# Broadcasts, Gram sums and the first chunk's spread on TensorE in a selective-scan block

## The chip, the cores and the metric

The kernel runs on one core of a Trainium2 chip. The metric is the device time of one execution in microseconds (us), the median of several runs.

## The reference

The input x is 8 batches of 96 channels by 64 x 64 positions (4096 tokens a batch). Two layers are computed:

```
u = group_norm(x, 32 groups)
xm, z = u @ in_proj.T                              # 192 channels each
xm = silu(causal depthwise conv of 4 taps (xm) + conv_b)
dt, Bm, Cm = xm @ x_proj.T                         # 6, 16 and 16 columns
delta = softplus(dt @ dt_proj_w.T + dt_proj_b)
h_t = exp(delta*A) * h_(t-1) + delta*u*Bm_t        # 192 channels x 16 states, over 4096 tokens
y_t = sum over states (h_t * Cm_t) + xm*D ;  x = x + layer_norm((y*silu(z)) @ out_proj.T)
t = x + attention(layer_norm(x))                   # without softmax, so through a Gram matrix
out = t + ffn(layer_norm(t))                       # hidden 384, operands in fp8, sums in f16
```

## The kernel before

**Tiling.** The 4096 tokens of each batch are 8 chunks of T = 512 tokens, so there are 64 chunks, numbered g = 0 to 63. The place of a chunk is g mod 8. The recurrence runs with 128 partitions = 32 channel groups x 4 states: the 192 x 16 pairs are 24 scans of 128 x 512 a chunk (L1277), in 6 quads s = 0 to 5 of 4 scans each. Quads 0 to 3 hold the "low" 128 channels, quads 4 and 5 the "high" 64.

**The work of one chunk.** ScalarE (ACT) computes a decay DA = exp(ds*A) for each scan (`decay`, L840) into one of two PSUM banks, so decay j can start only when scan j-2 is done. The scan's input D = us * B comes from `inputs`: VectorE (DVE) makes it for quads 0, 1 and part of 3 (L1261), GpSimd (POOL) for quads 2, 4, 5 (L649) and for the rest of quad 3 (`rest`, L658). SPLIT = 232 is the column at which quad 3 is divided. D has three buffers. Where DVE makes it, B stands in the PSUM bank PB, to which ACT copies it (`put_b`, L826, three copies a chunk). POOL then multiplies the scanned rows R with C (`product`, L676 and L672) and makes du = delta*u (L642). TensorE (PE) sums over the states into bank Y (`sum_states`, L1645 and L1649) and adds the skip (`add_skip`, L1656 and L1659); DVE gates (`gate`, L1298, in two halves).

**Through memory.** delta and du (tiles dl, du) and B, C (tile st) are produced on channel or state partitions, but the scans need them repeated over partitions. The DMA queue of SyncE (SP) writes them to scratch arrays in memory (lo_d, hi_d, bc_d) and reads them back repeated, into ds, us, Bs and Cs.

**Stages overlap.** An iteration g of every engine's program holds the scans of chunk g, the front of chunks g+1 and g+2 (norm, conv, `silu`, `x_proj`, `state_rows` L802 that copies x_proj's result from PSUM to st with a bias, `dt_proj`, `parts` L811, `softplus` L815, `delta` L1287), the layer norms of g-1 and g-2 (L851, L855, `scale_out` L1302, `token_norm` L1310), the Gram matrix of chunk g-2 (`gram`: PE multiplies the tokens tT with themselves, L1715, and DVE adds the result in bank G2 to tile G, L1336), and from g = 10 on the feed-forward of chunk g-10. One batch behind, `fold` turns the Gram sum into the attention's matrix. Each engine's order is written out by hand in `iteration`; semaphores tie them.

**The order that the change touches.** In iteration g, ACT goes: ... `decay(g,1,1)` (quad 1, scan 1), `decay(g,1,2)`, `state_rows(g+1)`, `decay(g,1,3)`, `output` (L929), `decay(g,2,0)`, two `parts`, `decay(g,2,1)`, `put_b(g,3)`, `softplus(g+1)`. DVE goes: `scan(g,0,0)`, `gate(g-1,0)`, `token_norm`, `scan(g,0,1)`, `inputs(g,1)`, `scan(g,0,2)`, `gate(g-1,1)`, `scan(g,0,3)`, `scan(g,1,0..2)`, `gram(g-2)`, `scan(g,1,3)`, `scan(g,2,0..1)`, `delta(g+1)`. PE goes: `add_skip(g-1,1)` (which waits for the first gate, L1659), `x2_tokens`, `sum_states(g-1,4)`, `sum_states(g-1,5)`, `to_tokens`, `x_proj(g+1)`, `down`, `gram(g-2)`, `dt_proj(g+1)`, `out_proj(g-1)`.

**The first chunk.** Nothing hides its front. ACT makes the low delta at 25 us, DVE clamps it (`delta`), SP writes it to lo_d as soon as it is there (L472, with semaphores low_out), POOL makes du, SP writes it too and reads both back spread (L488).

Of the kernel before, what the change touches and what calls it, by code (L numbers as in the profile page):

```python
# [9 lines left out]
T = 512  # L10
# [37 lines left out]
SPLIT = {3: 232}  # L48
# [8 lines left out]
def build(nc, I, cols, out):  # L57
# [7 lines left out]
    with ctx:  # L65
# [95 lines left out]

        once = pieces(stage[:, 1024:1024 + I["once"].shape[1]], cols["once"])
# [9 lines left out]
        wz, cb, dsk, wx, one_row, dtw = (W[n] for n in ("wz_in", "conv_b", "D", "wx", "one_row", "dtw"))  # L172
# [4 lines left out]
        off_group, of_group = W["off_group"], W["of_group"]  # L177
        wqT, wkv, wfT, b1f, b2f = (W[n] for n in ("wqT", "wkv", "wffT", "b1", "b2"))
        wcv = sb("wcv", [C, TAPS, 2 * LOW])
# [20 lines left out]
        un = sb("un", [C, HALO + T])  # L200
# [4 lines left out]
        st = sb("st", [128, T])  # L205
# [13 lines left out]
        sq = sb("sq", [C, T])  # L219
# [14 lines left out]
        fsq = sb("fsq", [C, T])  # L234
# [11 lines left out]
        w_in, w_rest, once_in, cwb_in = sem("w_in"), sem("w_rest"), sem("once_in"), sem("cwb_in")  # L246
# [5 lines left out]
        passed = sem("passed")  # L252
        x_in, xq_in = sem("x_in"), sem("xq_in")
# [4 lines left out]
        u_in = [sem("u_in0"), sem("u_in1")]  # L258
        first_quad = sem("first_quad")
# [4 lines left out]
        low_out = [sem("dl_low_out"), sem("du_low_out")]  # L264
# [9 lines left out]
        z_kept = sem("z_kept")  # L274
# [16 lines left out]
        post_dve = Progress("post_dve", 3)  # L291
# [104 lines left out]
        def _(sp_eng):  # L396
# [7 lines left out]
            sp_eng.dma_start(kept_w[:, 0:soon], I["kept"][:, 0:soon]).then_inc(w_in, 16)  # L404
            sp_eng.dma_start(stage[:, 1024:1024 + I["once"].shape[1]], I["once"]).then_inc(once_in, 16)
            sp_eng.dma_start(cwb, I["conv_w"].partition_broadcast(C)).then_inc(cwb_in, 16)

            def load_front(k):
                if there(k - 1):
                    sp_eng.wait_ge(front_mm.sem, front_mm.at(k - 1))  # L410
                    own_wait(sp_eng)
                t, lo = place(k) * T, 0 if place(k) == 0 else HALO
                sp_eng.dma_start(un[:, HALO - lo:HALO + T], I["x"][batch(k), :, t - lo:t + T]).then_inc(x_in, 16)
# [29 lines left out]
            def spill_bc(k):  # L443
                sp_eng.wait_ge(st_done.sem, st_done.at(k))
                if there(k - 2):
                    for n in range(2):
# [3 lines left out]
                                 st[32:32 + 2 * STATE, :]).then_inc(bc_out, 16)  # L450
# [30 lines left out]
            def spread(k, w, n, dst, landed):  # L481
                p = place(k) % 2
                if k == 0 and n == 0:
                    sp_eng.wait_ge(low_out[w], 16)
                else:
                    sp_eng.wait_ge(sp_out[w], count(k, 48, 48))
# [64 lines left out]
            def iteration(g):  # L551
# [5 lines left out]
                if there(g + 2):  # L557
                    load_front(g + 2)
# [11 lines left out]
                if there(g):  # L570
                    load_c(g, 1)
                if there(g + 1):
                    spill_bc(g + 1)
                    if g == -1:
                        load_b(0, 0)
                if ahead(g + 11):
                    load_stats(g + 11)
                if there(g + 1):
                    if g == -1:
                        first_spills()  # L580
                    else:
                        spill(g + 1, 0)
                        spill(g + 1, 1)
                    if g >= 0:
# [4 lines left out]
                    if g >= 0:  # L589
                        spread_delta(g + 1, 0)  # L590
                    load_b(g + 1, 1)
                    if g == -1:
                        load_c(0, 0)
# [28 lines left out]
        def _(pool):  # L622
            credit(nc.gpsimd, by_pool)

# [8 lines left out]
            def delta_u(k):  # L633
                if k == 0:
                    return first_delta_u()
                if k == 1:
                    pool.wait_ge(low_out[1], 16)
# [41 lines left out]
            def iteration(g):  # L679
                if there(g - 1):  # L680
                    product(g - 1, 5)
                if there(g):
                    if g == 0:
                        inputs(0, 1, first_quad)
# [26 lines left out]
        def _(act):  # L711
# [59 lines left out]
            def norm(k):  # L771
# [4 lines left out]
                if lo:  # L776
                    act.wait_ge(front_mm.sem, front_mm.at(k - 1))
                    nc.scalar.copy(un[:, 0:HALO], zero[0:C, 0:HALO])
                nc.scalar.activation(un[:, lo:], un[:, lo:], ACT.Identity, bias=cgs[:, 1:2],
                                     scale=cgs[:, 0:1]).then_inc(normed.sem, 1)  # L780

            def silu(k, *src):
# [14 lines left out]
            def state_rows(k, src):  # L797
                act.wait_ge(back_mm.sem, back_mm.at(k, 1))
                act.wait_ge(back_mm.sem, back_mm.at(k - 1))
                if there(k - 1):  # L800
                    act.wait_ge(bc_out, count(k - 1, 16, 16))
                nc.scalar.activation(st[:, :], src[:, :], ACT.Identity, bias=one_row).then_inc(st_done.sem, 1)  # L802

            def parts(k, v, src):
# [4 lines left out]
                if k == 1:  # L809
                    act.wait_ge(low_out[0], 16)  # L810
# [5 lines left out]

            def put_b(k, s):
                if k == 0 and s == 1:
                    return
                h, w = LOWS[s]  # L820
                if s == 3 and place(k + 3) == 0 and later(k + 3):
                    act.wait_ge(gn_act.sem, gn_act.at(k + 3, 4))
# [1398 lines left out]
```

## Time and profile before

| | |
|---|---|
| runs | 2509.95, 2510.44, 2512.78 us; median 2510.44 us |
| profiled execution, span from first to last instruction | 2508.8 us (its own device time is not listed; span and median lie 1.6 us apart) |
| granted TensorE clock, mean | 0.987 |
| busy PE, DVE, ACT, POOL | 2142.1, 2454.5, 2314.7, 2414.8 us |
| idle POOL before its first large operation | to 27.07 us |
| DMA | 494.54 MB, 197 GB/s |

A row of the timeline gives start, length, engine, line, operation, written tile <- read tiles, shapes and count; the bracket is the idle time of the engine before it and what ended it. The records of consecutive instructions on DVE, ACT and POOL overlap, so what one costs its engine is the distance from its start to the next start, somewhat less than its length.

### The profile page before, as it was taken

To read this page: it belongs to the slowest core of one execution; us is meant where nothing else is said; L and a number is where in the kernel's file an instruction comes from. 1 tells how busy PE (TensorE), PEld (TensorE's weight loads), DVE (VectorE), ACT (ScalarE), POOL (GpSimd) and SP (SyncE) were. 2 spreads that over 40 slices of the span, in tenths; PEclk is the share of its full clock that TensorE was granted. 3 is DMA by queue.
4 is the path that set the end of the run, shared out by engine and by line. 5 is a ranking of instruction groups with operands and counts; after the bars stand their busy time and mean duration, and the time that the engine had idled before them with its cause. 6 is when DMAs were issued, how large, how long until landed. Compare 5 with 4: busy or idle time off the path is not lost.

```text
span 2508.8 us, 35019 instructions
## 1 busy us (share of the span) xinstructions
PE 2142.1 (85%) x10314; PEld 826.0 (33%) x10314; DVE 2454.5 (98%) x2391; ACT 2314.7 (92%) x3960; POOL 2414.8 (96%) x655
## 2 busy tenths in 40 slices
PE   6788888888888888888888888888888888888878
PEld 3334434323323323323333323323323333333323
DVE  7999999999999999999999999999999999999986
ACT  5777777999999999999999999999999999999977
POOL 4999999999999999999999999999999999999991
PEclk8999999999999999999999999999999999999979
DMA  6555555556656656566566566566566565566542
GB/s 243 189 185 172 195 185 184 202 198 207 209 202 205 207 201 212 201 205 206 204 206 214 194 208 212 195 210 208 198 210 211 197 207 201 192 206 203 186 142 75
DMA packets 171388, 494.54 MB, mean 197 GB/s; under 512 B 23072, under 2 KB 44704, under 8 KB 154240
## 3 DMA queue, kind: packets, MB, share of 16 engines
q1 hardware_dynamic: 171200, 492.30, 57.9%
q8 instruction: 85, 1.39, 0.2%
q14 instruction: 103, 0.84, 0.1%
HBM read 400.33 MB, written 91.88 MB: 196 GB/s over the span
## 4 chain that ended last, share of the span: by engine, by line
POOL 40%; issue 40%; DVE 15%; PE 3%; ACT 1%; DMA 0%; POOLq 0%; DVEq 0%; SPq 0%; ACTq 0%
POOL R L676 20%; DVE R L1277 11%; POOL D L649 9%; POOL R L672 7%; POOL du L642 3%; DVE D L1261 2%; POOL D L658 2%; PE G L1568 1%; PE Y L1568 0%; DVE q L1357 0%; DVE dl L1287 0%; DVE G L1302 0%; DVE h L1471 0%; DVE h L1478 0%; PE Y L1645 0%
## 5 line engine op out<-in xcount | busy, mean ns | idle before, releaser
L1277 DVE TENSOR_TENSOR_SCAN R<-DA,R,D 128x512 f32<-128x512 f32 x1344 | 1630.2, 1263 | 1.0 <-ACT DA L840 1.0
L840 ACT ACTIVATE DA<-ds,kept_w 128x512 f32<-128x512 f32 x1536 | 1054.8, 688 | 139.9 <-DVE R L1277 127.1
L676 POOL TENSOR_TENSOR R<-R,Cs 128x2048 f32<-128x2048 f32 x255 | 970.9, 3819 | 4.0 <-DVE R L1277 2.6
L649 POOL TENSOR_TENSOR D<-us,Bs 128x2048 f32<-128x2048 f32 x193 | 736.9, 3818 | 8.8 <-DMA us<-lo_d 8.8
L672 POOL TENSOR_TENSOR R<-R,Cs 128x4096 f32<-128x4096 f32 x64 | 476.5, 7446 | 0.1
L1261 DVE TENSOR_TENSOR D<-us,PB 128x2048 f32<-128x2048 f32 x191 | 356.8, 1868 | 6.3 <-DMA us<-lo_d 6.3
L1645 PE MATMUL Y<-R,kept_w 128*32 128x512 f32 x2048 | 266.1, 615 | 13.9 <-POOL R L672 12.8
L1602 PE MATMUL G<-un,wcv 96*128 96x512 f32 x512 | 251.6, 614 | 29.5 <-ACT h L907 29.5
L1277 DVE TENSOR_TENSOR_SCAN R<-DA,D 128x512 f32<-128x512 f32 x192 | 221.7, 1204 | 2.1 <-ACT DA L840 2.1
L1605 PE MATMUL G<-un,wcv 96*64 96x256 f32 x1024 | 138.5, 392 | 60.1 <-ACT xq L888 58.9
L1568 PE MATMUL G<-st,kept_w 128*64 128x256 f32 (+1 forms) x384 | 108.9, 485 | 53.5 <-ACT st L802 53.5
L1602 PEld LDWEIGHTS G<-un,wcv 96*128 96x128 f32 x512 | 87.9, 189 | 187.8 <-issue 113.8
L1568 PE MATMUL G<-sq,kept_w 96*96 96x512 f32 (+1 forms) x256 | 136.7, 616 | 13.5 <-DVE dl L1287 12.6
L1649 PE MATMUL Y<-R,kept_w 128*32 128x256 f32 x2048 | 136.9, 385 | 5.9 <-POOL R L676 5.9
L658 POOL TENSOR_TENSOR D<-us,Bs 128x1120 f32<-128x1120 f32 x64 | 139.2, 2174 | 0.0
L1568 PE MATMUL G<-q,w1q 96*128 96x512 fp8e5 x164 | 62.7, 386 | 77.1 <-DVE q L1357 44.7
L911 ACT ACTIVATE h<-h,b1q 128x512 f16<-128x512 f16 x165 | 117.1, 711 | 0.0
L1605 PEld LDWEIGHTS G<-un,wcv 96*64 96x64 f32 x1024 | 62.3, 135 | 147.6 <-ACT xq L888 111.1
L1568 PE MATMUL G<-un,kept_w 96*64 96x256 f32 x372 | 107.9, 470 | 0.0
L1645 PEld LDWEIGHTS Y<-R,kept_w 128*32 128x32 f32 x2048 | 47.8, 110 | 168.3 <-issue 107.3
L642 POOL TENSOR_TENSOR du<-dl,u 128x768 f32<-128x768 f32 x63 | 97.6, 1549 | 0.0
L826 ACT COPY PB<-Bs 128x512 f32<-128x512 f32 x191 | 95.2, 498 | 0.0
(240 smaller groups left out, 3437.5 us busy)
## 6 DMA issues: line engine op xcount, KB each, us to landing
Bs<-bc_d SPq DMA_DIRECT2D x128, 512.0 KB, 5.6
us<-lo_d SPq DMA_DIRECT2D x64, 1024.0 KB, 6.3
ds<-lo_d SPq DMA_DIRECT2D x64, 1024.0 KB, 8.4
Cs<-bc_d SPq DMA_DIRECT2D x128, 512.0 KB, 4.7
us<-hi_d SPq DMA_DIRECT2D x64, 512.0 KB, 6.8
ds<-hi_d SPq DMA_DIRECT2D x64, 512.0 KB, 5.5
lo_d<-dl SPq DMA_DIRECT2D x64, 256.0 KB, 2.0
lo_d<-du SPq DMA_DIRECT2D x64, 256.0 KB, 2.0
```

Of the source, the lines that this page charges most:

```text
L642: nc.gpsimd.tensor_tensor(du[:, :], dl[:, :], u[:, place(k) % 2, :], ALU.mult)\
L649: nc.gpsimd.tensor_tensor(shaped(D[:, s % NDBU, :, :], s), low(us, s) if s in LOWS else high(us), of_states(Bs, s), ALU.mult).then_inc(don ...
L658: nc.gpsimd.tensor_tensor(D[:, s % NDBU, :, cs], us[:, 0:QUAD, cs], Bs[:, h, w, cs].unsqueeze(1).to_broadcast([128, QUAD, T - SPLIT[s]]), ...
L672: nc.gpsimd.tensor_tensor(R[:, s:s + 2, :, 0:T], R[:, s:s + 2, :, 1:S], Cs[:, 1, :, :].unsqueeze(2).to_broadcast([128, 2, QUAD, T]), ALU.m ...
L676: nc.gpsimd.tensor_tensor(shaped(R[:, s, :, 0:T], s), shaped(R[:, s, :, 1:S], s), of_states(Cs, s), ALU.mult).then_inc(hc_done.sem, 1)
L840: nc.scalar.activation(DA[j % NDA][:, :], ds[:, i, :], ACT.Exp, scale=A[:, j:j + 1]).then_inc(exp_done.sem, 1)
L1261: nc.vector.tensor_tensor(D[:, s % NDBU, :, 0:n], us[:, 0:QUAD, 0:n], PB[:, 0:n].unsqueeze(1).to_broadcast([128, QUAD, n]), ALU.mult)\
L1277: nc.vector.tensor_tensor_scan(R[:, s, q, 1:S], DA[j % NDA][:, :], D[:, s % NDBU, q, :], before, ALU.mult, ALU.add).then_inc(scanned.sem, 1)
L1568: return mm(o, left, right, start=True, stop=True)
L1602: last = mm(o[:, :], wcv[:, t, 0:LOW], un[:, t:t + T], start=(t == 0), stop=(t == TAPS - 1))
L1605: last = mm(o[rows, 0:H], wcv[:, t, LOW:LOW + HIGH], un[:, t + cs.start:t + cs.stop], start=(t == 0), stop=(t == TAPS - 1))
L1645: last = mm(Y[32 * q:32 * q + 32, :], sumsel, R[:, s, q, 0:T], start=s == 0, stop=s == 3)
```

## The change

1. `put_b` moves from ACT to PE: instead of copying the spread B from Bs, PE multiplies a selection matrix `bsel` (32 x 128) with the 32 state rows of st into PB. st gets two buffers, and its rows are laid out anew (B and C in rows 0 to 31, dt in rows 32 to 63, ones in row 64).
2. Four biases leave ACT: conv_b becomes a 97th row of the conv's first tap, the epsilon of the layer norms a 97th row of avg, and dt_proj's row of ones is set once, so `silu`, the Ln of L851 and L898, and `state_rows` run without a bias tile.
3. `gram`: PE first adds the old sum (identity `id97` times G) in PSUM, and ACT copies the result to G, behind `decay(g,1,2)`; DVE's addition goes (it stays for the last two chunks).
4. SPLIT: 232 becomes 248.
5. Chunk 0: low delta and du are spread by PE with 8 matmuls against four blocks of a selection matrix (`spread_first`), and ACT copies each result to ds or us; the two early spills and the two spreads through memory go. DVE makes D of quad 0 scan by scan. Quad 1's D is POOL's, as before. z of chunk 0 gets its Silu early, `silu(1)` moves behind `decay(0,1,1)`, `z_proj(1,0)` into iteration 0, and two of the six statistics of batch 2 behind `scan(0,2,1)`. SP's order at the start follows.

```diff
-SPLIT = {3: 232}
+SPLIT = {3: 248}
...
 # SyncE
+            sp_eng.dma_start(wcv[C:C + 1, 0, :], I["conv_b"]).then_inc(cb_in, 16)
...
-                for w, low_done, src in ((0, dl_low, dl), (1, du_low, du)):
-                    sp_eng.wait_ge(low_done, 1)
-                    sp_eng.dma_start(lo_d[0, w].rearrange("e i t -> (e i) t"), src[:, part(0)]).then_inc(low_out[w], 16)
...
                     if g == -1:
                         load_b(0, 0)
+                        load_b(0, 1)
...
-                    spread_du(g + 1, 0)
-                    if g == -1:
-                        spread_delta(0, 0)
...
 # ScalarE
-                nc.scalar.activation(st[:, :], src[:, :], ACT.Identity, bias=one_row).then_inc(st_done.sem, 1)
+                nc.scalar.copy(st[0:64, k % 2, :], src[0:64, :]).then_inc(st_done.sem, 1)
...
-            def put_b(k, s):
...
-                nc.scalar.copy(PB[:, 0:n], Bs[:, h, w, 0:n]).then_inc(b_put.sem, steps_to(k, s))
...
+            def gram(k, src):
+                act.wait_ge(post_mm.sem, post_mm.at(k, 6))
+                if place(k) == 0 and there(k - CH):
+                    act.wait_ge(fold_mm.sem, fold_mm.at(k - CH, 1))
+                nc.scalar.copy(G[:, :], src[0:C + 1, 0:C + 1]).then_inc(gram_kept.sem, 1)
...
                 if there(g):
                     decay(g, 1, 2)
+                if there(g - 2) and g - 2 < LAST - 1:
+                    gram(g - 2, G2)
                 if there(g + 1):
                     state_rows(g + 1, G3)
...
+                keep_ds(0, 1, Y)
                 decay(0, 0, 0)
+                keep_us(0, 2, G2)
+                keep_ds(1, 3, G3)
+                decay(0, 0, 1)
+                keep_us(1, 4, G0)
+                keep_us(2, 5, Y)
+                keep_us(3, 6, G2)
+                keep_ds(2, 7, G3)
+                decay(0, 0, 2)
+                keep_ds(3, 8, G0)
...
 # VectorE
+            def first_inputs(q):
...
+                nc.vector.tensor_tensor(D[:, 0, q, :], us[:, q, :], PB[:, :], ALU.mult)\
+                    .then_inc(first_d if q + 1 < QUAD else dbu_d.sem, 1)
...
-                if there(g - 2):
-                    gram(g - 2, G2)
...
+                if g == 0:
+                    stats(2, gx_in[3:4], range(4, 6))
...
 # TensorE
             def gram(k, o):
+                more = place(k) > 0 and k < LAST - 1
+                if more:
+                    pe.wait_ge(gram_kept.sem, gram_kept.at(k - 1))
+                    mm(o[0:C + 1, 0:C + 1], id97, G[:, :], start=True, stop=False)
...
+            def put_b(k, s):
...
+                pe.wait_ge(st_done.sem, st_done.at(k))
+                pe.wait_ge(dbu_d.sem, dbu_d.at(k, BY_DVE[s] - 1))
+                n = SPLIT.get(s, T)
+                one(PB[:, 0:n], bsel[:, BY_DVE[s] - 1, :], st[0:2 * STATE, k % 2, 0:n]).then_inc(b_put.sem, 1)
...
+                if there(g):
+                    put_b(g, 1)
                 if there(g - 1):
                     add_skip(g - 1, 1)
...
                     out_proj(g - 1, G1)
+                if there(g):
+                    put_b(g, 3)
...
                     variance(g - 1, 1, G2)
+                if there(g + 1):
+                    put_b(g + 1, 0)
...
+                put_b(0, 0)
...
+                pe.wait_ge(dl_low, 1)
+                spread_first(dl, 0, Y)
+                pe.wait_ge(du_low, 1)
+                pe.wait_ge(w_ready, 1)
+                spread_first(du, 0, G2)
+                spread_first(dl, 1, G3)
...
+            def spread_first(src, q, o):
+                one(o[:, :], of_block[:, q, :], src[:, part(0)]).then_inc(picked, 1)
```

## Rows read from the trace of the kernel before

**Rows 1.** Busy time by engine, chunks 11 to 60 (columns: stretch, length, engines, clock, DMA)

```profile
core 0: us, PE busy (x) PEld busy (x) DVE busy (x) ACT busy (x) POOL busy (x), PEclk, DMA share, GB/s
380.00:2390.00 2010.00, 1732.14 (x8393) 646.71 (x8381) 2007.10 (x1908) 1952.32 (x3354) 2006.90 (x537) 1.00 0.60 203
```

**Rows 2.** DVE's waits: from 120 to 430 us, and from 430 to 1500 us

```profile
DVE yv L1298 <- PE Y L1649: 3.3, 7, 0.8
...
DVE G L1302 <- ACT rs L855: 1.0, 4, 0.2
```

**Rows 3.** POOL's timeline: the same operation of chunks 40 and 48, a batch apart

```profile
1518.95 1.54 POOL L642 TENSOR_TENSOR du<-dl,u 128x768 f32<-128x768 f32 x1
...
1819.38 1.55 POOL L642 TENSOR_TENSOR du<-dl,u 128x768 f32<-128x768 f32 x1
```

**Rows 4.** Groups by shape from 500 to 2000 us (busy us, mean ns of one)

```profile
L1261 DVE TENSOR_TENSOR D<-us,PB 128x2048 f32<-128x2048 f32 x80 | 180.6, 2258 | 0.0
...
L649 POOL TENSOR_TENSOR D<-us,Bs 128x2048 f32<-128x2048 f32 x120 | 458.5, 3821 | 0.0
```

**Rows 5.** DVE's timeline in iteration 43, a common one

```profile
1662.61 0.23 DVE L1336 TENSOR_TENSOR G<-G 97x97 f32<-97x97 f32 x1
1662.76 3.62 DVE L1277 TENSOR_TENSOR_SCAN R<-DA,R,D 128x512 f32<-128x512 f32 x3
```

**Rows 6.** ACT's timeline in the same iteration

```profile
1660.37 0.69 ACT L840 ACTIVATE DA<-ds,kept_w 128x512 f32<-128x512 f32 x1 [0.46 <-DVE R L1277]
1661.00 0.67 ACT L802 ACTIVATE st<-G,kept_w 128x512 f32<-128x512 f32 x1
1661.57 0.68 ACT L840 ACTIVATE DA<-ds,kept_w 128x512 f32<-128x512 f32 x1
...
1664.15 0.69 ACT L840 ACTIVATE DA<-ds,kept_w 128x512 f32<-128x512 f32 x1
1664.76 0.36 ACT L826 COPY PB<-Bs 128x232 f32<-128x232 f32 x1
1665.04 0.85 ACT L815 ACTIVATE dl<-dl 128x768 f32<-128x768 f32 x1
```

**Rows 7.** PE's timeline in the same iteration

```profile
1650.40 1.13 PE L1568 MATMUL G<-un,kept_w 96*128 96x512 f32 x2
1652.55 0.65 PE L1659 MATMUL Y<-u,kept_w 64*64 64x256 f32 x4 [1.02 <-DVE yv L1298]
...
1660.19 0.85 PE L1715 MATMUL G<-tT 128*97 128x97 f32 x8
```

**Rows 8.** Groups of ACT by shape from 500 to 2000 us: copies and small operations from PSUM

```profile
L888 ACT COPY xq<-G 96x512 f32<-96x512 f32 x40 | 23.8, 594 | 0.0
...
L744 ACT ACTIVATE gt<-PB 96x1 f32<-96x1 f32 x5 | 0.8, 159 | 0.0
```

**Rows 9.** Timelines of PE and of DVE in iteration 40, place 0

```profile
1547.67 0.85 PE L1715 MATMUL G<-tT 128*97 128x97 f32 x8
...
1549.80 0.23 DVE L1336 TENSOR_TENSOR G<-G 97x97 f32<-97x97 f32 x1
```

**Rows 10.** Timelines of PE and of DVE in iteration 45, place 5

```profile
1735.71 0.91 PE L1715 MATMUL G<-tT 128*97 128x97 f32 x8
...
1737.73 0.23 DVE L1336 TENSOR_TENSOR G<-G 97x97 f32<-97x97 f32 x1
```

**Rows 11.** PE's timeline at the start

```profile
24.91 0.57 PE L1568 MATMUL PB<-kept_w 96*97 96x192 f32 x2
```

**Rows 12.** DVE's timeline at the start

```profile
26.30 1.02 DVE L1287 SCALAR_TENSOR_TENSOR dl<-dl,G 128x512 f32<-128x512 f32 x2
...
37.55 2.29 DVE L1261 TENSOR_TENSOR D<-us,PB 128x2048 f32<-128x2048 f32 x1 [6.31 <-DMA us<-lo_d]
40.72 10.14 DVE L1277 TENSOR_TENSOR_SCAN R<-DA,D 128x512 f32<-128x512 f32 x9 [0.89 <-ACT DA L840]
```

**Rows 13.** POOL's timeline at the start

```profile
37.59 7.59 POOL L649 TENSOR_TENSOR D<-us,Bs 128x2048 f32<-128x2048 f32 x2 [8.84 <-DMA us<-lo_d]
...
55.05 1.55 POOL L642 TENSOR_TENSOR du<-dl,u 128x768 f32<-128x768 f32 x1
```

More of the change, by code:

```diff
@@ L482, in spread @@
                 p = place(k) % 2
[L483 to L486, printed above, removed]
+                sp_eng.wait_ge(sp_out[w], count(k, 48, 48))
                 if n == 0:
@@ L556, in iteration @@
                     load_c(g, 0)
-                if there(g + 2):
+                if there(g + 2) and g != 0:
                     load_front(g + 2)
@@ L787, in silu @@
                     act.wait_ge(front_mm.sem, front_mm.at(k, FRONT[v]))
-                    nc.scalar.activation(u[:, place(k) % 2, part(v)], src[v], ACT.Silu, bias=cb[:, v:v + 1])\
+                    nc.scalar.activation(u[:, place(k) % 2, part(v)], src[v], ACT.Silu)\
                         .then_inc(silued.sem, 1)
@@ L935, in iteration @@
             def iteration(g):
-                if there(g):
-                    put_b(g, 1)
+                if there(g) and g > 0:
                     decay(g, 0, 1)
@@ L940, in iteration @@
                     inv_std(g - 2, 1)
-                if there(g):
+                if there(g) and g > 0:
                     decay(g, 0, 2)
@@ L1031, in iteration @@
                     decay(g, 5, 0)
-                if there(g + 1):
-                    put_b(g + 1, 0)
                 if g == LAST:
@@ L1096, in beginning @@
                     act.wait_ge(front_mm.sem, front_mm.at(0, 1 + v))
-                    last = nc.scalar.activation(u[:, 0, part(v)], src[:, 0:T - H * v], ACT.Silu, bias=cb[:, v:v + 1])
-                    last.then_inc(silued.sem, 1)
+                    nc.scalar.activation(u[:, 0, part(v)], src[:, 0:T - H * v], ACT.Silu).then_inc(silued.sem, 1)
+                for v in range(2):
+                    act.wait_ge(front_mm.sem, front_mm.at(0, 3 + v))
+                    nc.scalar.activation(z[:, 0, part(v)], DA[v][:, 0:T - H * v], ACT.Silu).then_inc(silued.sem, 1)
                 nc.scalar.preload_act_table_set(EXP_LN)
@@ L1101, in beginning @@
                 state_rows(0, G0)
-                for v in range(2):
-                    act.wait_ge(front_mm.sem, front_mm.at(0, 3 + v))
-                    nc.scalar.copy(z[:, 0, part(v)], DA[v][:, 0:T - H * v]).then_inc(z_kept, 1)
                 norm(1)
@@ L1202, in stats @@
                     dve.wait_ge(gn_aggr.sem, gn_aggr.at(CH * n - CH))
-                for c in range(ROW // T):
+                for c in blocks:
                     if c % per == 0:
@@ L1374, in iteration @@
                     scan(g, 0, 1)
+                if there(g) and g > 0:
                     inputs(g, 1)
+                if there(g):
                     scan(g, 0, 2)
@@ L1419, in iteration @@
                     scan(g, 5, 1)
-                if there(g + 1):
+                if there(g + 1) and g >= 0:
                     inputs(g + 1, 0)
```

243 lines of the change are left out of this document (138 added, 105 removed).

## The prediction

> **What bounds the kernel now.** First the busy time by engine of the long middle: POOL and DVE are both busy 2007 of 2010 us, ACT 1952, PE 1732, at full clock [rows 1]. Neither of the two waits for memory, so the question is which sets the pace. The waits answer it by stretch: up to chunk 10 DVE stalls at its gate L1298, seven times and 3.3 us in all, for sums that wait for POOL's products; from there on its only waits are 1.0 us in 29 chunks, for ACT's rs [rows 2]. So POOL sets the pace of some 11 chunks and DVE that of the 53 behind them. The distance of one POOL operation over a batch says how close it is: 1819.38 - 1518.95 = 300.4 us [rows 3], where eight chunks in which POOL never waits would take about 299.5 (its seven of 3.8, the pair and the two small ones, 37.44 each).
>
> At the start nothing of this holds: DVE waits 6.31 us and POOL 8.84 us for us from memory, and POOL's unbroken work begins at 37.59 [rows 12, 13].
>
> **The third engine** matters because DVE waits for its decays. In a common iteration ACT idles 0.46 us before the decay at 1660.37, since there are two banks [rows 6]; from that point its order is tied to DVE's scans. Its next decay starts at 1661.57 and ends at 1662.25, and the scan that reads it starts at 1662.76, behind the Gram addition [rows 5, 6]. The slack is 0.5 us. The change takes 0.15 of it from DVE's side and puts a wait for PE into ACT's.
>
> **The change, part by part.** I sum against the profiled execution's span, 2508.8 us; the same difference is then laid on the median, 2510.4.
>
> *Split at 248.* 16 columns of 4 rows, 64 elements, go from POOL to DVE. By [rows 4] an element costs POOL 3821/2048 = 1.87 ns and DVE 2258/2048 = 1.10 ns: -0.12 us for POOL, +0.07 for DVE, each chunk.
>
> *Gram addition off DVE.* From its start to the next start it costs 0.15 us [rows 5]. With the split: -0.08 us a chunk for DVE.
>
> *Gram sum on PE and ACT.* PE adds two passes of 97 columns; eight take 0.85 us, the record of one alone being about 0.25, so 0.086 each, +0.17 [rows 7]. PE's Gram product ends at 1661.04 and would end at 1661.21; ACT, free at 1661.00, would begin to copy at 1661.25 (about 0.04 between the engines, estimated from the gaps of such rows). The copy of 97 columns appears nowhere: it is above one of 1 column (record 0.16) and below one of 512 (0.59) [rows 8]; consecutive records overlap by 0.1, and on the line between both it takes 0.24 - 0.1 = 0.14, ends 0.06 and 0.49. I take 0.13. `state_rows` follows at 1661.38. It costs 0.57 now (1661.00 to 1661.57); without a bias tile it is a copy like L888, whose record is 0.59 against 0.67, so 0.48. Then the decay starts at 1661.86, ends at 1662.55, and the scan could start at 1662.58; DVE without its addition gets there at 1662.61. No stall. Two decays on, ACT has no pause any more: in the present row it takes 2.58 us from decay to decay (1661.57 to 1664.15), of which about 0.1 is a wait that goes, so the decay at 1664.15 would start at 1664.32, and its scan at 1665.05. DVE gets there at 1664.97 (two scans of 1.18 behind 1662.61): a stall of **0.07 us** in a common chunk, which eats nearly all of the 0.08.
>
> That ACT is quicker without the bias is also what the Trainium skill says (ScalarE: Activation LUTs, What ACT_TABLE_LOAD costs): a [128,1] pointer operand adds some 93 ns. The rows agree (0.67 against 0.59). By the page's slope of 0.833 ns a column and the 51 ns it gives for PSUM (Perfetto Trace Analysis, Optimizing Scalar/DVE Operations) the copy of G would be an estimated 0.13 us; the sum above does not need it.
>
> *The same reading elsewhere in a batch.* Place 0: scans without a carried start are 0.05 shorter, the product ends at 1548.52, the addition stood at 1549.80 [rows 9]: 1548.52+0.17+0.04+0.13+0.48+0.73 = 1550.07, a stall of 0.27, and 0.21 more two decays on; 0.48. Place 5: group-norm matmuls for the next batch stand ahead of the product, which ends at 1736.62; 1738.17 against 1737.73 is 0.44 [rows 10], and with the small Ln behind it and the second stall 0.67. For places 1 and 2, whose product is late by less, I put 0.3 and 0.2. With four common chunks at 0.07 that is **1.9 us a batch** (ends: 0 if ACT copies while PE is early, and 3 if the copy takes 0.25).
>
> *B on PE.* The three copies leave ACT; one stands between decay and softplus, 0.28 us from start to start [rows 6]. DVE's waits for rs, 1.0 us in 29 chunks [rows 2], should vanish with it and the cheaper Ln: -0.3 us a batch. PE gains two pairs of 512 columns and one of 248, and its queue is the question. The nearest row is a pair that starts at 1650.40; PE stands idle 1.02 us up to 1652.55, waiting for DVE's gate [rows 7]. A pair of 1.0 us ahead of `add_skip` fills that idle time to within 0.1. `put_b(g,3)` (0.45) delays a variance that waits for DVE anyhow, `put_b(g+1,0)` stands before two waits of PE for ACT of 0.5 us each. I take 0 for all, ends 0 and +0.25 a chunk.
>
> *The first chunk.* Now: `put_b(0,0)` goes ahead of the fold's matmul at 24.91 [rows 11], for which DVE waits before its clamp, so delta moves from 26.30 to about 27.3 [rows 12]. Then come eight pairs on PE at 1.0 us from about 28.2, each followed by an ACT copy of about 0.55, with three decays of 0.7 between. The last piece of us is the seventh thing ACT does, after PE's sixth pair (34.3): us is whole at about 35.0. POOL begins there and not at 37.59: -2.6. DVE begins its scans at about 32 instead of 40.72 but then loses 3.6 us, since `silu(1)` and its two table loads (1.28 us each) now stand between two decays; this lies beside POOL's two large operations (7.6 us [rows 13]). `delta(1)` moves behind two statistics and is late by some 0.6 for POOL's L642 at 55.05. Left: **-2.2 us** (ends: -0.5, if us waits on B's load or PE is slower; -3.5). The spills and spreads saved were 2.5 MB that nobody else waited for.
>
> *Sum.* Start -2.2. 11 chunks at POOL's pace, -0.12 each: -1.3. 53 chunks, 6.6 batches, at DVE's: -0.08 x 53 = -4.2; waits for rs -2.0; stalls for ACT +1.9 x 6.6 = +12.5. Together +2.8 us. The end of the kernel is as before: its last two Gram additions stay on DVE. 2510.4 + 2.8 = 2513.2, **2513 us**.
>
> **Rivals.** *(A) No new stall worth naming.* If ACT's copy slips in while PE's product is early, or the decay chain has more play than I read, the 12.5 us fall to 0 to 5: 2510.4 - 2.2 - 1.3 - 4.2 - 2.0 = 2500.7, up to 2505. For it: the common chunk misses by only 0.07; ACT loses 1.3 us of copies and 0.5 us of biases a chunk. Against it: places 0 and 5 miss by 0.3 and more. *(B) PE's queue, slower.* `put_b(g,1)` stands ahead of `add_skip(g-1,1)`, and from there to the Gram product PE has no pause. Should the pair cost over 1.1 us (weights not loaded in time, for instance), every tenth beyond delays both the second gate and ACT's copy. At +0.25 us a chunk over 53 chunks: +13, 2525; it decides from 1.1 us on, and +0.1 gives 2518. For it: the idle time is 1.02 us, no more. Against it: pairs in this stretch follow each other at 1.0. *(C) The start brings nothing*, since POOL's early work is tied to scans behind `silu(1)`: 2514.5; inside the forecast.
>
> **How the numbers follow.** A measurement of this kernel tells 0.2%, 5 us, from no change. The forecast and C, 2505.5 to 2515.5: 0.45 (C 0.07 of it). Rival A, below: 0.33. B, or stalls near 3 us a batch (2520), above: 0.22. Neither side alone can be left out; the range reaches to A's time and to B's lower half: 2500 to 2519.
>
> **What would show it.** In the changed profile: ACT's L802 (now a copy) 0.09 shorter, and about 0.4 us later behind its decay; DVE's waits with "R <- ACT DA" of about 0.07 in common chunks, 0.3 or more at places 0 and 5, some 12 us in all; POOL waiting for DVE's scans 2 to 3 us a batch; a batch 0.9 us longer than 300.4 (-0.66 - 0.3 + 1.9); us whole at 35 and POOL's first L642 near 52.8. No such DVE waits, and batches near 299.5, would be A. PE without its idle time before L1659, and DVE waiting for L1649, would be B.

## The result, and the profile after

| | before | after |
|---|---|---|
| median of 4 runs each (us) | 2510.39 (2509.95 to 2512.78) | 2529.90 (2527.32 to 2534.85) |
| ratio | | 1.0077, interval 1.0062 to 1.0091 |
| profiled execution: span | 2508.8 | 2526.5 (its device time 2528.29) |
| a batch in the steady part (defined below) | 300.43 | 302.77 |

The change makes the kernel slower by 0.8%, and the time lies above the predicted range. (Before now has a fourth run, 2510.34 us, beside the three listed above.) Below, a batch is always the distance between the starts of DVE's `token_norm` of chunks 24 and 56, divided by four. Lines have moved: the decay is L825, the scan L1290, `scale_out` L1315, the Ln and Exp of rs L836 and L840, the selection products of `put_b` L1582 with PB.

The busy time of the long middle, to be held against [rows 1]:

```profile
380.00:2390.00 2010.00, 1857.83 (x8766) 697.35 (x8765) 1996.42 (x1838) 1870.08 (x3224) 1983.71 (x532) 1.00 0.61 202
```

PE has taken over 126 us and ACT has lost 82, as the change means it to. But DVE is idle 13.6 us and POOL 26.3 us, where both had 3 before; no engine has work in every microsecond any more. The clock is full, so it is no matter of clock. The waits of the same stretch as [rows 2], 430 to 1500 us, say who waits for whom (total, times, longest), first DVE's, then POOL's:

```profile
DVE R L1290 <- ACT DA L825: 2.5, 8, 0.5
DVE G L1315 <- ACT rs L840: 1.2, 4, 0.3
...
POOL R L670 <- DVE R L1290: 13.9, 27, 1.1
```

POOL is faster than its data: it waits for DVE's scans in nearly every chunk. DVE waits for ACT, for decays and for rs. This view leaves out pauses too short to count as a wait, so the next step is to look at the steps of DVE in all chunks of a batch. A step between two starts is 1.19 us for a scan; what it takes beyond that is a stall. Before the scans of quads 1 and 2 these stalls sum to 1.84 us a batch (0.08 in common chunks, 0.54 at place 0, 0.23 at place 1, 0.67 at place 5). Before `scale_out` they sum to 1.75 us a batch (0.21 in nearly every chunk), against 0.49 before the change. The first sum was predicted (1.9). The second was predicted to vanish. Together they explain the batch: 1.84 for decays, 1.26 more for rs and -0.64 for the split and the Gram addition make 2.46, against 2.33 measured.

**The decays.** ACT's timeline in iteration 43, the chunk of [rows 5 to 7]:

```profile
1671.79 0.69 ACT L825 ACTIVATE DA<-ds,kept_w 128x512 f32<-128x512 f32 x1 [0.46 <-DVE R L1290]
1672.66 0.24 ACT L875 COPY G<-G 97x97 f32<-97x97 f32 x1 [0.18 <-PE G L1740]
1672.80 0.58 ACT L796 COPY st<-G 64x512 f32<-64x512 f32 x1
1673.27 0.69 ACT L825 ACTIVATE DA<-ds,kept_w 128x512 f32<-128x512 f32 x1
...
1680.49 0.59 ACT L836 ACTIVATE rs<-G 96x512 f32<-96x512 f32 x1 [0.27 <-PE G L1582]
1680.98 0.68 ACT L825 ACTIVATE DA<-ds,kept_w 128x512 f32<-128x512 f32 x1
1681.59 0.62 ACT L840 ACTIVATE rs<-rs 96x512 f32<-96x512 f32 x1
```

The first four rows are the prediction's working come true: the pause of 0.46 is still there, the copy waits for PE (0.18), costs 0.14 (predicted 0.13), `state_rows` costs 0.47 (predicted 0.48), and the decay behind them stands 1.48 us behind the one before, where [rows 6] had 1.20. The last three rows are what the prediction missed: a new wait of 0.27 us for PE ahead of the Ln.

**The rs.** What PE does up to that Ln, in the same iteration:

```profile
1671.60 0.34 PE L1734 MATMUL G<-G,kept_w 97*97 97x97 f32 x2
1671.77 0.85 PE L1740 MATMUL G<-tT 128*97 128x97 f32 x8
1673.52 1.68 PE L1582 MATMUL G<-st,kept_w 65*128 65x512 f32 x6 [0.90 <-ACT st L796]
...
1677.02 0.68 PE L1582 MATMUL PB<-st,kept_w 32*128 32x248 f32 x2
1677.63 1.10 PE L1794 MATMUL G<-tn,MT 97*96 97x512 f32 x2
1678.57 1.02 PE L1797 MATMUL G<-xt,kept_w 96*96 96x512 f32 x2
1679.43 1.02 PE L1582 MATMUL G<-sq,kept_w 97*96 97x512 f32 x2
1680.37 1.07 PE L1582 MATMUL G<-fsq,kept_w 97*96 97x512 f32 x2
```

and in the kernel before, where the variance (L1568 of sq) had a pause ahead of it:

```profile
1661.81 1.68 PE L1568 MATMUL G<-st,kept_w 128*128 128x512 f32 x6 [0.78 <-ACT st L802]
...
1667.34 1.10 PE L1568 MATMUL G<-sq,kept_w 96*96 96x512 f32 x2 [0.23 <-DVE dl L1287]
```

Counted from the decay ahead of `state_rows` (1671.79 after, 1660.37 before), `dt_proj` starts at 1.73 instead of 1.44, because ACT's `state_rows` is late by the Gram copy; `put_b(g,3)` takes 0.61 (1677.02 to 1677.63); and the variance starts at 7.64 instead of 6.97. The pause of 0.23 for dl is used up. 0.29 + 0.61 - 0.23 = 0.67: the sum closes. ACT's Exp starts at 9.80, where it stood at 9.49 (1669.86), so rs is ready at 10.42. DVE could begin `scale_out` at 10.24, the distance it has before the change (1670.61) and in the first kernel below, which has the same decay stalls and no wait for rs; so it waits for rs. DVE's timeline:

```profile
1680.84 1.28 DVE L1290 TENSOR_TENSOR_SCAN R<-DA,R,D 128x512 f32<-128x512 f32 x1
1682.24 0.75 DVE L1315 SCALAR_TENSOR_TENSOR G<-G,kept_w,rs 96x512 f32<-96x512 f32 x1
```

1.40 us from start to start, 0.21 more than a scan costs.

**The start.** POOL, to be held against [rows 13]:

```profile
34.81 7.58 POOL L643 TENSOR_TENSOR D<-us,Bs 128x2048 f32<-128x2048 f32 x2 [4.87 <-ACT us L1120]
...
52.21 1.54 POOL L636 TENSOR_TENSOR du<-dl,u 128x768 f32<-128x768 f32 x1 [0.27 <-issue]
```

POOL begins at 34.8 (predicted 35.0) and is 2.8 us ahead at du of chunk 1, 52.21 against 55.05 (predicted 2.2). It does not keep this. DVE waits 3.48 us behind `silu(1)` (predicted 3.6), and then in iteration 1 PE runs warm-up products at half clock. PE, ACT and DVE there:

```profile
89.03 3.65 PE L1582 MATMUL G<-kept_w 128*128 128x256 f32 x8
92.51 1.02 PE L1582 MATMUL G<-sq,kept_w 97*96 97x512 f32 x2
93.38 1.03 PE L1582 MATMUL G<-kept_w 128*128 128x256 f32 x4
```

```profile
93.57 0.59 ACT L836 ACTIVATE rs<-G 96x512 f32<-96x512 f32 x1 [3.65 <-PE G L1582]
```

```profile
95.33 0.75 DVE L1315 SCALAR_TENSOR_TENSOR G<-G,kept_w,rs 96x512 f32<-96x512 f32 x1 [3.17 <-ACT rs L840]
```

Eight passes take 3.48 us from start to start, four passes right behind them 0.95: the first are at the lower of the two clock levels, the others at the higher (the granted clock from 80 to 100 us is 0.83, a mean of both). The variance stands behind them in the queue. DVE waits 3.17 us for rs behind it, and du of chunk 3 is only 0.2 us earlier than before the change. In the profiled execution of the kernel before, the eight passes of this place took 1.95 us.

**Where the 17.7 us of span came from**, read off POOL's du of each chunk, after minus before: -2.8 at chunks 1 and 2, -0.2 at chunk 3, -0.1 at chunk 10, +16.7 at chunk 63, +17.7 at the end of the span. (The 1.0 us behind chunk 63 is within the scatter: that tail takes 126.5 us before, 127.5 after, and 124.8 to 130.3 in the profiled executions of all kernels here.) So the chunks up to 10 bring nothing where -3.5 was predicted, and the 53 behind them +16.8 where +6.3 was predicted.

### The profile page after: what moved, and what is told of

Same layout as the page of the kernel before. It is cut to its first block, busy times and chain, and to the rows that moved or that the text cites. A ratio compares the mean times of both kernels' runs of the same rounds, so it can differ in the third digit from the quotient of the medians.

```text
span 2526.5 us, 35808 instructions
## 1 busy us (share of the span) xinstructions
PE 2314.8 (92%) x10820; PEld 894.6 (35%) x10820; DVE 2461.0 (97%) x2333; ACT 2234.9 (88%) x3838; POOL 2409.7 (95%) x659
## 4 chain that ended last, share of the span: by engine, by line
PE 50%; DVE 35%; issue 7%; ACT 6%; POOL 0%; DVEq 0%; DMA 0%; ACTq 0%; SPq 0%; POOLq 0%
DVE R L1290 27%; PE G L1582 11%; PE Y L1670 5%; DVE D L1265 4%; PE PB L1582 3%; PE G L1622 3%; PE Y L1666 3%; PE G L1641 2%; PE G L1685 2%; PE G L1812 2%; PE G L1643 2%; PE G L1804 2%; PE G L1687 2%; PE G L1794 2%; PE G L1740 2%
## 5 line engine op out<-in xcount | busy, mean ns | idle before, releaser
L1290 DVE TENSOR_TENSOR_SCAN R<-DA,R,D 128x512 f32<-128x512 f32 x1344 | 1632.0, 1264 | 5.6 <-ACT DA L825 4.3
L825 ACT ACTIVATE DA<-ds,kept_w 128x512 f32<-128x512 f32 x1536 | 1056.7, 688 | 196.2 <-DVE R L1290 192.3
L1265 DVE TENSOR_TENSOR D<-us,PB 128x992 f32<-128x992 f32 x190 | 358.9, 1889 | 0.2 <-DVE R L1290 0.2
L1622 PE MATMUL G<-un,wcv 96*128 96x512 f32 (+1 forms) x512 | 252.8, 616 | 0.0
L1290 DVE TENSOR_TENSOR_SCAN R<-DA,D 128x512 f32<-128x512 f32 x192 | 222.4, 1205 | 6.6 <-ACT DA L825 5.8
L1625 PE MATMUL G<-un,wcv 96*64 96x256 f32 (+1 forms) x1024 | 138.3, 391 | 66.9 <-ACT xq L879 66.9
L1582 PE MATMUL PB<-st,kept_w 32*128 32x512 f32 x382 | 187.3, 570 | 0.5 <-DVE D L1265 0.5
L1582 PE MATMUL G<-st,kept_w 65*64 65x256 f32 (+1 forms) x384 | 107.5, 480 | 57.7 <-ACT st L796 57.7
L1622 PEld LDWEIGHTS G<-un,wcv 96*128 96x128 f32 (+1 forms) x512 | 87.4, 189 | 156.0 <-issue 116.5
L1582 PE MATMUL G<-sq,kept_w 97*96 97x512 f32 (+1 forms) x256 | 132.1, 597 | 0.5 <-ACT h L898 0.5
L652 POOL TENSOR_TENSOR D<-us,Bs 128x1056 f32<-128x1056 f32 x64 | 131.7, 2058 | 0.0
L1625 PEld LDWEIGHTS G<-un,wcv 96*64 96x64 f32 (+1 forms) x1024 | 62.3, 136 | 154.9 <-ACT xq L879 119.0
L1582 PE MATMUL G<-q,w1q 96*128 96x512 fp8e5 x164 | 63.1, 388 | 50.5 <-DVE q L1366 47.1
L1582 PE MATMUL G<-un,kept_w 96*64 96x256 f32 x378 | 108.8, 468 | 0.0
L1582 PEld LDWEIGHTS PB<-st,kept_w 32*128 32x128 f32 x382 | 56.2, 184 | 122.1 <-issue 122.1
```

Of the source, the lines that this page charges most:

```text
L652: nc.gpsimd.tensor_tensor(D[:, s % NDBU, :, cs], us[:, 0:QUAD, cs], Bs[:, h, w, cs].unsqueeze(1).to_broadcast([128, QUAD, T - SPLIT[s]]), ...
L825: nc.scalar.activation(DA[j % NDA][:, :], ds[:, i, :], ACT.Exp, scale=A[:, j:j + 1]).then_inc(exp_done.sem, 1)
L1265: nc.vector.tensor_tensor(D[:, s % NDBU, :, 0:n], us[:, 0:QUAD, 0:n], PB[:, 0:n].unsqueeze(1).to_broadcast([128, QUAD, n]), ALU.mult)\
L1290: nc.vector.tensor_tensor_scan(R[:, s, q, 1:S], DA[j % NDA][:, :], D[:, s % NDBU, q, :], before, ALU.mult, ALU.add).then_inc(scanned.sem, 1)
L1582: return mm(o, left, right, start=True, stop=True)
L1622: last = mm(o[:, :], wcv[0:rows_of(t), t, 0:LOW], un[0:rows_of(t), t:t + T], start=(t == 0), stop=(t == TAPS - 1))
```

## The experiments

All kernels are the changed one with the edit shown. "Before" is the unchanged kernel on the same chip.

**Whose wait is it? One product moved.** `put_b(g,3)` goes ahead of `dt_proj(g+1)` (but for place 5, where it must stay behind group-norm work).

```diff
 # TensorE, iteration
+                if there(g) and not (place(g + 3) == 0 and later(g + 3)):
+                    put_b(g, 3)
...
-                if there(g):
+                if place(g + 3) == 0 and later(g + 3):
                     put_b(g, 3)
```

> The changed kernel with one step of TensorE moved: put_b(g,3) stands ahead of dt_proj, where TensorE idles 0.9 us in the changed kernel's trace, instead of behind out_proj (only in chunks of place 5 it stays). Theory Q (TensorE's queue: the 0.6 us of this product make variance(g-1,0) late, so ACT's Ln and Exp are late and VectorE waits before scale_out, 0.21 us in every chunk): the wait 'DVE G <- ACT rs' goes, some 1.3 us a batch, 2530 falls to 2520 to 2522. Theory G (the loss is ACT's copy of the Gram sum, and the waits for rs are only where it shows): no change, 2528 to 2532.

Measured: 2512.6 (before 2512.47; 10 runs, 2510.99 to 2526.53), ratio 1.0016, interval 0.9999 to 1.0033; a batch 301.07. The product stands in a pause that PE has anyway, its wait for st. PE in the same iteration (the decay is at 1662.38):

```profile
1663.14 0.68 PE L1582 MATMUL PB<-st,kept_w 32*128 32x248 f32 x2
1664.11 1.68 PE L1582 MATMUL G<-st,kept_w 65*128 65x512 f32 x6 [0.28 <-ACT st L796]
...
1669.29 1.10 PE L1582 MATMUL G<-sq,kept_w 97*96 97x512 f32 x2
```

The variance is back at 6.91. DVE's waits from 430 to 1500 us are now those for decays alone, unchanged to the tenth:

```profile
DVE R L1290 <- ACT DA L825: 2.5, 8, 0.5
```

So the rs waits hang on PE's queue, and the decay stalls don't. The time fell by some 8 us more than theory Q said. The wait that went is 1.70 us a batch, x 6.6 = 11.2 us. Between the two profiled spans lie 15.4 us, by POOL's du 12.3 of them in chunks 11 to 63, 1.2 before and 1.9 behind; the first chunks and the tail differ from execution to execution (below).

**More of the same product.** From chunk 10 on the product of `put_b(g,3)` is issued twice.

```diff
 # TensorE, put_b
+                if s == 3 and k >= 10:
+                    one(PB[:, 0:n], bsel[:, BY_DVE[s] - 1, :], st[0:2 * STATE, k % 2, 0:n])
```

> The changed kernel with the product of put_b(g,3) issued twice from chunk 10 on (the same operands into the same bank; the output is the same). Theory Q: variance(g-1,0) comes another 0.5 us later, and VectorE's wait for rs grows by that in nearly every one of 53 chunks: 25 us more, about 2555. If TensorE's queue has play behind this point, 2530 as before.

Measured: 2551.56, ratio 1.0154, interval 1.0137 to 1.0171; a batch 306.09. DVE's waits from 430 to 1500 us:

```profile
DVE G L1315 <- ACT rs L840: 15.4, 28, 0.7
DVE R L1290 <- ACT DA L825: 2.5, 8, 0.5
```

PE in iteration 43 (the decay is at 1686.95):

```profile
1692.18 1.10 PE L1582 MATMUL PB<-st,kept_w 32*128 32x248 f32 x4
1693.21 1.10 PE L1796 MATMUL G<-tn,MT 97*96 97x512 f32 x2
```

The doubled product takes 1.03 us from start to next start, where the single one took 0.61: 0.42 more on PE. It costs 3.32 us a batch, 0.42 a chunk, all of it before `scale_out`; the decay stalls stay as they are. What PE's queue gets late there, DVE pays in full: that chain has no slack left in the changed kernel.

**The copies back on ACT.** In this kernel `put_b` is a copy by ACT again, at its three places of before; all else stays, but for a semaphore that `state_rows` waits for.

```diff
 # ScalarE
+            def put_b(k, s):
...
+                nc.scalar.copy(PB[:, 0:n], Bs[:, h, w, 0:n]).then_inc(b_put.sem, 1)
 # TensorE
-                if there(g):
-                    put_b(g, 1)
...
-                if there(g):
-                    put_b(g, 3)
...
-                if there(g + 1):
-                    put_b(g + 1, 0)
```

> The changed kernel with all three copies of B back on ACT, as in the kernel before; Gram sum, biases, split and start stay as changed. Theory Q: TensorE's idle times return, the wait for rs falls from 1.75 to about 0.5 us a batch, 2522. Theory G: ACT has 1.3 us a chunk more to do in its chain, so the stalls for decays grow, 2532 or more.

Measured: 2513.35, ratio 1.0002, interval 0.9992 to 1.0011; a batch 301.47. ACT's wait for PE before the Ln is gone, and the decay stalls did not grow (2.5 us, 8 times, as before this edit). DVE still waits 0.55 us a batch for rs, the level of before, since ACT has its three copies again. So moving `put_b` to PE, good for ACT, cost 1.3 us a batch net where it was put. The wait for rs came out as theory Q said; the time is 9 us below its 2522, more than the batches explain, and the first chunks of this execution kept their gain (du of chunk 3 is 2.7 us early).

**The Gram addition back on DVE.** For place 0 DVE copies the product and so begins the sum.

```diff
 # ScalarE
-                if there(g - 2) and g - 2 < LAST - 1:
-                    gram(g - 2, G2)
 # VectorE, iteration
+                if there(g - 2) and g - 2 < LAST - 1:
+                    gram(g - 2, G2)
 # TensorE, gram
-                more = place(k) > 0 and k < LAST - 1
+                more = False
```

> The changed kernel with the Gram addition back on VectorE (behind scan(g,1,2)) and without TensorE's identity product. Theory G: the stalls of VectorE for decays (1.8 us a batch) go, and since dt_proj starts 0.3 us earlier the wait for rs as well (1.3), against 1.2 us of additions: 1.9 us a batch less, about 2517. Theory Q alone: the variance stays late by 0.6, VectorE pays 0.15 a chunk and gains only the stalls, 2526.

Measured: 2510.53, ratio 0.9991, interval 0.9982 to 1.0; a batch 300.31. DVE has no wait from 430 to 1500 us. Both the decay stalls and the rs waits go, as theory G said, and the batch is 0.6 us shorter than it said, in part because the additions cost less than 1.2 us (below). ACT still waits for PE before its Ln, as this group says, from 500 to 2000 us of this kernel:

```profile
L836 ACT ACTIVATE rs<-G 96x512 f32<-96x512 f32 x80 | 46.6, 583 | 6.7 <-PE G L1586 6.7
```

but less than in the changed kernel, whose group is

```profile
L836 ACT ACTIVATE rs<-G 96x512 f32<-96x512 f32 x80 | 46.7, 584 | 9.3 <-PE G L1582 9.3
L875 ACT COPY G<-G 97x97 f32<-97x97 f32 x39 | 9.4, 242 | 11.2 <-PE G L1740 10.7
```

and DVE itself comes 0.15 later. The rs wait has two parents: the product ahead of the variance, and the Gram copy ahead of `state_rows`, which makes st late for `dt_proj`. The last row also shows what the copy costs besides its own time: 11.2 us in 39 chunks in which ACT waits for PE's Gram product.

**The Gram copy one decay later.** If the copy's place is at fault and not the copy, ACT can do it behind `decay(g,1,3)`:

```diff
 # ScalarE
                     decay(g, 1, 2)
-                if there(g - 2) and g - 2 < LAST - 1:
-                    gram(g - 2, G2)
...
                     decay(g, 1, 3)
+                if there(g - 2) and g - 2 < LAST - 1:
+                    gram(g - 2, G2)
```

> The changed kernel with ACT's copy of the Gram sum one step later: behind decay(g,1,3) instead of between decay(g,1,2) and state_rows(g+1), so that ACT does not wait for TensorE there. My theory (two costs that share one cause: what stands between decay(g,1,2) and state_rows delays the decays and, through dt_proj, everything behind it on TensorE, the variance for rs included): the stalls for decays go (1.8 us a batch) and most of the waits for rs too (1.3), a batch of 299.4 us instead of 302.8, 2508 to 2511. If the two costs are independent: the waits for rs stay, 301 us a batch, 2518.

Measured: 2504.1 (before 2511.26), ratio 0.9963, interval 0.995 to 0.9976; a batch 299.40. It beats both kernels. ACT in iteration 43:

```profile
1653.91 0.69 ACT L825 ACTIVATE DA<-ds,kept_w 128x512 f32<-128x512 f32 x1 [0.46 <-DVE R L1290]
1654.54 0.57 ACT L796 COPY st<-G 64x512 f32<-64x512 f32 x1
1655.08 0.69 ACT L825 ACTIVATE DA<-ds,kept_w 128x512 f32<-128x512 f32 x1
1655.71 0.23 ACT L875 COPY G<-G 97x97 f32<-97x97 f32 x1
```

The copy does not wait for PE, and the next decay stands 1.17 us behind the one before instead of 1.48, and `state_rows` starts before it without a pause. The long middle, again as [rows 1], and the only waits that the view shows there from 430 to 1500 us, DVE's and POOL's:

```profile
380.00:2390.00 2010.00, 1878.71 (x8807) 702.17 (x8809) 2008.97 (x1859) 1887.83 (x3260) 2006.60 (x539) 1.00 0.61 204
```

```profile
DVE G L1315 <- ACT rs L840: 0.5, 3, 0.2
...
POOL R L670 <- DVE R L1290: 0.2, 1, 0.2
```

DVE is busy but for 1.0 us of 2010. The decay stalls are gone from this view (by the steps 0.2 us a batch is left, at places 0 and 5), and so are most of the rs waits, although `put_b(g,3)` stands where it stood. In the same iteration the variance starts 7.25 us behind the decay, 0.28 later than before the change, and DVE does not wait. So neither the product nor the late `dt_proj` alone brings the wait for rs in a common chunk; together, at 7.64, they do.

**Both moves.** The Gram copy late and `put_b(g,3)` early:

> Both single moves together: put_b(g,3) ahead of dt_proj on TensorE, the Gram copy behind decay(g,1,3) on ACT. My theory: nothing is left for VectorE to wait for, a batch of 299.2 us against 300.4 before; with the start some 8 us below the kernel before, 2503 to 2506. Rival (GpSimd or the fold becomes the limit, or the start's gain is not kept): 2508 to 2511.

Measured: 2504.39, ratio 0.9976, interval 0.9963 to 0.9989 (10 runs, 2500.65 to 2515.5); a batch 299.41. Once the copy is late, the product's place is worth nothing, since DVE's own work fills the batch. The same with the addition on DVE and `put_b(g,3)` early:

> put_b(g,3) ahead of dt_proj, and the Gram addition on VectorE. My theory: no waits are left, but VectorE pays 0.15 us a chunk for the addition: 300.1 us a batch, 2508 to 2510, that is 4 to 6 us above the version with the late copy.

Measured: 2507.28, ratio 0.9996, interval 0.9976 to 1.0015 (10 runs, 2505.32 to 2523.01); a batch 300.26. So DVE's Gram addition costs 300.26 - 299.41 = 0.85 us a batch where nothing else is in the way, against 8 x 0.15 = 1.2 by its row [rows 5]. (Two intervals here are wide; the batch lengths, from the profiles, are what separates these kernels.)

**The split.** SPLIT back at 232, in the changed kernel and in the one with the late copy, and the latter with 248 once more beside it:

```diff
-SPLIT = {3: 248}
+SPLIT = {3: 232}
```

> The changed kernel with the split back at 232 and nothing else. What is the split worth where it stands? The sum put -0.12 us a chunk on POOL and +0.07 on DVE. If DVE's own work still sets the pace of the steady chunks (302.77 us a batch), it gains 8 x 0.07 = 0.56 a batch: 302.2, 2529.9 - 3.7 + 1.3 (the early chunks at POOL's pace) = about 2527.5. Rival: DVE waits in every chunk for decays and for rs, so its end of an iteration is fixed by ACT and PE, and a shorter input addition only lengthens a wait: batch 302.77 within 0.1, 2530 to 2531. POOL has 13.9 us of waits in 27 chunks and can take 0.12 more without being felt in either case.

> ACT's Gram copy behind decay(g,1,3) and the split back at 232. With the copy moved and the split at 248 a batch took 299.40, POOL's own floor by the prediction's working (299.5), with no wait of POOL from 120 us on. If POOL sets that pace, 0.12 a chunk more for it gives 300.4 a batch, +6.3 over the 53 chunks and +1.3 in the early ones: 2504.1 + 7.6 = 2511.7. If DVE still sets it, 298.8 a batch and about 2501.

> The same kernel as e6_gram_late (the Gram copy behind decay(g,1,3), split 248), beside the one with 232 and on its chip, so that the two can be compared and the gain over the kernel before is measured a second time: ratio 0.996 to 0.9975, 2504 us, batch 299.4. If the first measurement was luck of the early stage, it comes out at 0.998 or above.

Measured, before at 2512.03: in the changed kernel 2525.63, ratio 1.0058 (1.0044 to 1.0072), a batch 302.55; with the late copy and 232, 2507.36, ratio 0.9982 (0.9973 to 0.999), a batch 299.55; with the late copy and 248, 2503.39, ratio 0.9965 (0.9951 to 0.9979), a batch 299.43. In the changed kernel DVE's shorter addition (L1265, 1092 ns against 1161) gives 0.22 us a batch where its own 0.07 a chunk would be 0.56: most of it becomes a longer wait for rs. The median is below what either theory gave (2527.5 and 2530), by more than 0.22 us a batch can do; the four runs go from 2522.95 to 2531.49. With the late copy the view of the long middle for 232 reads

```profile
380.00:2390.00 2010.00, 1877.68 (x8802) 702.48 (x8804) 2004.93 (x1859) 1885.89 (x3258) 2010.00 (x538) 1.00 0.61 204
```

POOL is busy 2010 of 2010 us and a batch takes 299.55: that is POOL's floor at 232, which the prediction had put at 299.5. My expectation of 300.4 for this kernel was wrong: it took 299.4 for POOL's floor at 248, while POOL had 3.4 us of idle time there and DVE 1.0. At 248 DVE sets the pace, at 232 POOL, and the two differ by 0.15 us a batch. The batches explain 0.15 x 6.6 = 1 us of the 4 between the medians, and chunks 3 to 10, which gain 0.9 us against before at 248 and 0.1 at 232, another 0.8. The two profiled spans, 2505.3 and 2501.6 us, lie 3.7 apart, and 2.7 of that arise behind POOL's du of chunk 63, where the tail takes 129.5 us in the first and 126.8 in the second, at a granted clock of 0.74 against 0.86 in its stretch from 50 to 70 us. So most of the 4 us is seen in the tail and not in the chunks; that the split causes it is not shown.

**The warm-up products.** Is the start's gain lost to them? They are taken out around the variance in iterations 1 to 9:

```diff
 # TensorE
-                if 0 < g < 10:
...
-                    spin(2, G2, *weights)
...
-                if 0 < g < 10:
-                    spin(2, G2, *weights)
```

> The changed kernel without the warm-up products (8 passes of 256 columns) that stand between put_b(g,3) and variance(g-1,0) in iterations 1 to 9; they compute nothing that is used. In the changed kernel's trace they take 3.65 us at half clock in iteration 1, and VectorE waits 3.2 us for rs there, which takes back the 2.8 us that the start had won. Theory S (these products are what gives the start's gain back): 2.5 to 4 us less, 2526. Rival: without them TensorE's clock stays low for longer and the time is the same or worse.

Measured: 2541.96, ratio 1.0093, interval 1.0057 to 1.0129; a batch 302.77. The loss at iteration 1 is gone (du is still 2.8 us early at chunk 5), and far more is lost behind it. Two stretches of this kernel:

```profile
200.00:280.00 80.00, 73.59 (x335) 30.91 (x334) 71.46 (x65) 52.66 (x90) 72.37 (x20) 0.89 0.52 173
280.00:360.00 80.00, 74.38 (x334) 31.11 (x330) 72.12 (x66) 52.89 (x88) 72.72 (x20) 0.89 0.53 172
```

The clock is at 0.89 in each, and each costs 7.3 us in POOL's du; the longest waits of DVE there, 4.3 and 4.1 us, are for the sums in Y. It does not seem to happen every time: three of the five runs lie at 2542 to 2546 with a mean clock of 0.98, the other two took 2522.19 and 2528.22 with 0.991 and 0.988, below the changed kernel's median. By the median the warm-up is worth more than it takes. The same loss can come with the warm-up in place: the profiled run of the kernel with both moves has clock 0.91 from 280 to 380 us, and POOL's du falls back by 6.7 us there.

That the 2.6 us of iteration 1 hang on the clock too is seen in two executions of one kernel, the one with the late copy. From 80 to 100 us, the first and the second, each with the eight passes and the variance behind them:

```profile
80.00:100.00 20.00, 17.30 (x82) 8.50 (x76) 19.41 (x19) 14.45 (x25) 18.11 (x7) 1.00 0.34 111
...
88.87 1.99 PE L1582 MATMUL G<-kept_w 128*128 128x256 f32 x8
90.70 1.02 PE L1582 MATMUL G<-sq,kept_w 97*96 97x512 f32 x2
```

```profile
80.00:100.00 20.00, 17.30 (x57) 8.55 (x56) 16.82 (x17) 12.34 (x21) 18.66 (x7) 0.83 0.36 122
...
89.01 3.65 PE L1582 MATMUL G<-kept_w 128*128 128x256 f32 x8
92.50 1.02 PE L1582 MATMUL G<-sq,kept_w 97*96 97x512 f32 x2
```

The eight passes take 1.83 us in the first and 3.49 in the second. From chunk 2 to chunk 3 POOL's du loses nothing in the first and 2.6 us in the second. At chunk 3 it is 1.5 us ahead of before in the first, which had already lost 1.1 us at chunk 2, and 0.2 us in the second.

## Why the prediction was wrong, point by point

1. *Split, Gram addition off DVE, -0.08 a chunk.* The sizes are right (POOL's rest 2058 ns against 2176, DVE's 1161 against 1093), and with the late copy they are had: 299.40 against 300.43 a batch, -1.03 where the prediction had -0.66 for them and -0.3 for rs.
2. *The copy, state_rows, the stalls for decays, 1.9 us a batch.* Right: 0.14, 0.47 and 1.84.
3. ***B on PE: "waits for rs should vanish: -0.3 us a batch" and "`put_b(g,3)` (0.45) delays a variance that waits for DVE anyhow ... I take 0".*** **This is the step that failed.** The waits for rs did not fall to 0.19 or below but rose from 0.49 to 1.75 us a batch. The product was put at nothing because that variance waits anyhow; it waited 0.23 us, and the product takes 0.61, not 0.45. Its predecessor `dt_proj` was late by 0.29 for the very Gram copy that the prediction had costed for the decays and not for st. -0.3 predicted, +1.26 measured, 1.56 x 6.6 = **10.3 us**, about the 10.5 by which the 53 chunks were off (by the batch lengths, 2.33 against 0.94, it is 9.2). Moving that one product removes 1.70 a batch, doubling it adds 3.32. The product alone would have passed in a common chunk, as the late copy shows: it took both delays.
4. *Eleven chunks, -1.3.* From chunk 3 to chunk 10 they came to +0.1. With either single move (the product early, the copy late) the same chunks bring -0.8 to -0.9, so they are at POOL's pace only as long as DVE is not late, and in the changed kernel it is.
5. *The start, -2.2.* Came (-2.8) and was given back to 0.2 at chunk 3, by half-clock warm-up in iteration 1 ahead of the same variance. That is bad luck in part: in another execution of a kernel with the same start the clock was full there. Points 4 and 5 together are 3.4 us. Another 1 us lies behind chunk 63, and the median is 1.6 us above the profiled execution.
6. *Rival B* had the right engine and the wrong place. `put_b(g,1)` fits ahead of `add_skip`: it starts at 1662.76, the gate ends at 1663.90 and the skip starts at 1663.96, so the skip still waits for the gate and nobody for the skip. The queue overflowed 14 us later, at `put_b(g,3)`. Its size was about right for the 53 chunks: 1.56 us a batch is 0.2 a chunk, within its 0.1 to 0.25. Even its upper end lay short of 2529.9 because the gains of points 4 and 5 were counted as kept. By its own sum that end is 2513.2 + 13.2 = 2526.4, not 2525. Rival C likewise comes to 2515.4 by the sum, not 2514.5.
7. *Rival A*, "no new stall", is what the late copy makes: batches of 299.4 and 2504 us, where A had "near 299.5" and 2500.7 to 2505. But that is another kernel; of the changed one A was wrong.

What stays open: why the clock of the first 100 us differs between executions of one kernel, how much of the spread of the times hangs on that, and whether the split has any part in the tail of 232 against 248.

## What to carry to other kernels

"It waits anyhow" hides an insertion only up to the length of that wait, 0.23 us here against 0.61, plus the play of what follows: read the wait's length in the row and follow everything behind it in the queue to the engine that sets the pace. Here a variance 0.28 us late cost nothing and one 0.67 late cost 0.21. Delays that each fit must be added before they are called free. When an operation is put ahead of another on an in-order engine, list every reader of what now comes later: the Gram copy delayed the decays, which was costed, and st, which was not. And an operation that nobody needs soon (G, one chunk later) goes behind the ones that the pace-setting engine waits for: one line moved turned +0.8% into -0.4%.

## What the runs showed of the hardware

A product with 32 rows of contraction is no cheaper than one with 128: the pair of 512 columns from `bsel` has records of 1.12 us for two passes, the skip with 128 rows 1.13. A 97x97 copy out of PSUM costs ACT 0.14 us, a 64x512 one 0.47. At the lower clock, eight passes of 256 columns took 3.48 us and four at the higher 0.95, 0.43 against 0.24 a pass. Which of the two an execution has between 80 and 100 us changed between two executions of one kernel (granted clock 1.00 and 0.83). Without the eight passes the clock fell in two later stretches of the profiled execution, 7.3 us each; two of its five runs were no slower than the changed kernel.
